# Last norm normalised on ScalarE, and other products that keep TensorE busy, in a perceiver layer kernel

## The reference

```python
x = x + xattn(_layernorm(x), ctx, ctx)    # 16 heads, 2048 context rows per batch, softmax
x = x + attn(_layernorm(x))               # gated scan over the tokens, state 64
x = x + ffn(_layernorm(x))                # 8 experts, top 2 of 8, and 2 shared experts

def _layernorm(x, axis=-1, eps=1e-05):
    m = jnp.mean(x, axis=axis, keepdims=True)
    v = jnp.var(x, axis=axis, keepdims=True)
    return (x - m) / jnp.sqrt(v + eps)
```

## Time and profile before

| | |
|---|---|
| time, median of 3 runs | 521.34 us (521.06 to 521.61) |
| the profiled execution | 521.11 us |
| its span, first to last instruction | 519.3 us |
| mean granted clock of TensorE | 0.974 |
| TensorE busy | 483.9 us (93%) |
| VectorE busy | 403.6 us (78%) |
| ScalarE busy | 332.4 us (64%) |
| POOL busy | 274.8 us (53%) |

### The profile page before, as it was taken

One profiled execution on the slowest core, in us unless ns is written; L12 is line 12 of the kernel. 1 busy time (PEld: TensorE's weight loads), 2 busy tenths in 40 slices (PEclk: granted clock), 3 DMA queues, 4 the chain that ended last, 5 costly groups with the idle time before them and its releaser, 6 DMA issues.

```text
span 519.3 us, 16078 instructions
## 1 busy us (share of the span) xinstructions
PE 483.9 (93%) x6871; PEld 343.7 (66%) x6871; DVE 403.6 (78%) x611; ACT 332.4 (64%) x371; POOL 274.8 (53%) x262
## 2 busy tenths in 40 slices
PE   4999879889999999999989999998999999999994
PEld 4456656566766676776766559645787878787642
DVE  3757867678877788878758787787899999989426
ACT  3356677567767668766575267464788988878310
POOL 0438887998999999999960213461010111100051
PEclk9759989999999999999999999999999999999998
DMA  6998957899897988889989220278999999997144
GB/s 225 245 290 229 248 155 230 237 269 251 208 272 247 265 261 259 221 223 319 328 314 359 74 82 2 66 258 326 394 366 416 418 419 418 416 414 290 40 122 142
DMA packets 29822, 133.99 MB, mean 258 GB/s; under 512 B 6452, under 2 KB 6708, under 8 KB 18996
## 3 DMA queue, kind: packets, MB, share of 16 engines
q1 hardware_dynamic: 26072, 120.91, 71.6%
q0 software_dynamic: 3680, 12.06, 6.4%
HBM read 96.77 MB, written 11.01 MB: 208 GB/s over the span
## 4 chain that ended last, share of the span: by engine, by line
PE 54%; DVE 29%; issue 8%; DMA 4%; POOL 2%; ACT 2%; SPq 0%; DVEq 0%; ACTq 0%; POOLq 0%
DVE ws L832 10%; PE bank L1096 9%; PE bank L1156 9%; DVE mx L766 8%; PE bank L1141 7%; PE bank L1165 6%; DMA wst<-in_ffw 3%; PE bank L1231 3%; PE bank L1309 2%; PE bank L1307 2%; PE bank L1308 2%; POOL ps L682 2%; PE bank L1173 2%; DVE hf L1012 2%; DVE hl L1017 2%
## 5 line engine op out<-in xcount | busy, mean ns | idle before, releaser
L766 DVE TENSOR_REDUCE mx<-bank 128x1 f32<-128x512 f32 x240 | 154.9, 686 | 53.9 <-PE bank L1096 52.0
L508 ACT ACTIVATE pt<-bank 128x1024 f32<-128x1024 f32 x128 | 124.4, 1023 | 56.9 <-PE bank L1141 50.6
L682 POOL TENSOR_TENSOR ps<-pt 128x512 f32<-128x512 f32 x120 | 149.6, 1272 | 1.0 <-ACT pt L508 0.5
L832 DVE SCALAR_TENSOR_TENSOR ws<-wst,ws 128x2048 f16<-128x2048 f32 x51 | 116.7, 2309 | 2.6 <-ACT ws L564 2.5
L564 ACT ACTIVATE ws<-wst 128x2048 f16<-128x2048 f32 x48 | 90.5, 1904 | 5.0 <-DMA wst<-in_ffw 4.7
L1322 PE MATMUL bank<-xt,ws 128*128 128x128 f16 x480 | 81.2, 219 | 0.8 <-DVE hf L1012 0.8
L1324 PE MATMUL bank<-xt,ws 128*128 128x128 f16 x480 | 81.2, 219 | 0.0
L1323 PE MATMUL bank<-xt,ws 128*128 128x128 f16 x480 | 81.2, 219 | 0.0
L723 POOL DMA_DIRECT2D ys_rows<-xn x15 | 8.1, 543 | 121.4 <-ACT xn L639 121.4
L658 POOL TENSOR_TENSOR kl<-kt,kh 128x512 f16<-128x512 f32 x58 | 67.3, 1182 | 9.1 <-ACT kh L454 6.8
L1156 PE MATMUL bank<-pt,v 128*32 128x128 f32 x2048 | 70.0, 276 | 2.2 <-issue 2.2
(11 more groups left out here) (190 smaller groups left out, 763.5 us busy)
## 6 DMA issues: line engine op xcount, KB each, us to landing
wst<-in_ffw SPq DMA_DIRECT2D x51, 1024.0 KB, 10.8
kt<-in_keysT SPq DMA_DIRECT2D x16, 1024.0 KB, 6.2
v<-in_vals SPq DMA_DIRECT2D x16, 1024.0 KB, 9.1
kstk<-kh SPq DMA_DIRECT2D x88, 128.0 KB, 4.7
kstk<-kl SPq DMA_DIRECT2D x44, 128.0 KB, 3.2
wst<-kh SPq DMA_DIRECT2D x40, 128.0 KB, 4.7
xs_rows<-biases SPq DMA_DIRECT2D x15, 256.0 KB, 7.7
x_tok<-xs_rows POOLq DMA_DIRECT2D x15, 256.0 KB, 8.8
```

The costliest lines, as they stand in the source:

```text
L508: act.activation(pt[:, n % 4, :, :, :].rearrange("p j a t -> p (j a t)"), bank[:, 2 * (n % 2):2 * (n % 2) + 2, :].rearrange("p j n -> p (j ...
L682: pool.tensor_tensor(ps2[:, n % 4, :, :], pt[:, n % 4, 0, :, :], pt[:, n % 4, 1, :, :], ALU.add)\
L766: dve.tensor_reduce(mx[:, a, q:q + 1], bank[:, 4 + k % 2, :], AX.X, ALU.max).then_inc(m_taken, 1)
L832: dve.scalar_tensor_tensor(ws[:, home_of(q), 1, m, :, :].rearrange("p c n -> p (c n)"), wst[:, q % 2, m, :, :].rearrange("p c n -> p (c n) ...
```

## The change

The last norm's tile is no longer made by VectorE. VectorE computes the reciprocal of the root and, in a new small operation, minus the mean times it, and signals a new semaphore. A new function normalise(b) on ScalarE waits for it and computes the tile as Identity(scale * x2 + bias), both columns per token. It stands in ScalarE's list at the end of round b of the loop, behind root(b), take_residual(b + 2), in the last round the load of the exponent table, and copy_high(b - 1). The idle products ahead of the transposes go from 10, 6, 6 to 6, 3, 5. And in quarter 0 of group 2, between a tile of max scores and the first scores, TensorE does seven products of ones to a bank whose maxima have been taken.

```diff
@@ -601,6 +602,11 @@
             act.wait_ge(scan_out, b + 1)
             act.activation(x2[:, b, :], bank[:, 4 + b, :], ACT.Copy, scale=1.0 / WS).then_inc(x2_done, 1)
 
+        def normalise(b):
+            act.wait_ge(third_set, b + 1)
+            act.activation(xn[:, b, :], x2[:, b, :], ACT.Identity, bias=lnv[:, 3, b:b + 1],
+                           scale=lnv[:, 2, b:b + 1]).then_inc(h3_done, 1)
+
         take_residual(0)
         take_residual(1)
         for b in range(B):
@@ -611,6 +617,7 @@
                 act.activation(r1[:, 2, 0:2], eps[:, :], ACT.Exp)
             if b > 0:
                 copy_high(b - 1)
+            normalise(b)
         copy_high(B - 1)
@@ -920,8 +927,8 @@
         def third_norm(b):
             dve.wait_ge(roots, 11 + b)
             link(dve.reciprocal(lnv[:, 2, b:b + 1], lnv[:, 0, b:b + 1]))
-            dve.tensor_scalar(xn[:, b, :], x2[:, b, :], mv[:, b, 0:1], lnv[:, 2, b:b + 1], ALU.subtract,
-                              ALU.mult).then_inc(h3_done, 1)
+            dve.scalar_tensor_tensor(lnv[:, 3, b:b + 1], mv[:, b, 0:1], -1.0, lnv[:, 2, b:b + 1], ALU.mult,
+                                     ALU.mult).then_inc(third_set, 1)
@@ -1168,9 +1175,9 @@
-        def keep_busy(count):
+        def keep_busy(count, n=7):
             for _ in range(count):
-                pe.matmul(bank[:, 7, 0:P], one[:, :], one[:, :], start=True, stop=True)
+                pe.matmul(bank[:, n, 0:P], one[:, :], one[:, :], start=True, stop=True)
@@ -1187,6 +1194,10 @@
                 if p == 1 and a == 1 and i + 2 < G:
                     queries(i + 2)
+                if i == 2 and p == 0 and a == 0:
+                    j, k = tenants[1]
+                    pe.wait_ge(m_taken, MB * j + k - 1)
+                    keep_busy(7, 4 + k % 2)
                 scores(n)
@@ -1341,7 +1352,7 @@
             if b < 3:
-                idle_products(3, (10, 6, 6)[b])
+                idle_products(3, (6, 3, 5)[b])
             transpose_tokens(b)
```

More of the change, by code:

```diff
@@ L263, in build_program @@
     idw_done = sem("scaled_identity_done")
+    third_set = sem("third_norm_factors")
     x2_done = sem("x2_done")
```

## The result

| | before | after |
|---|---|---|
| time, median of 6 runs | 521.2 us (519.38 to 521.82) | 525.4 us (523.68 to 528.78) |
| ratio | 1 | 1.0091, 95% interval 1.0059 to 1.0123 |
| the profiled execution | 521.11 us | 524.64 us |
| its span | 519.3 us | 522.9 us |
| TensorE, VectorE, ScalarE, POOL busy | 483.9, 403.6, 332.4, 274.8 us | 482.4, 401.5, 335.3, 274.7 us |

The change makes the kernel slower by 0.9%, 4.7 us by the ratio, 4.2 us between the medians. I had said 524.3 us (522.3 to 526.4), so the time lies in the range, 1.1 us above the forecast.

A forecast was written before the change was run, and what follows sets the result against it. The chain from the last norm through TensorE and VectorE's router was taken to bound the end; 521.11 + 2.1 (ring and table load) + 0.9 (clock) + 0 = 524.1, 524.3 us on the median's scale, range 522.3 to 526.4.

The forecast's parts named there:

- The ring and the table load: Last norm: ScalarE's normalise waiting on copy_high and transposes, plus the exponent table load, make batch 3's transposes 2.1 us later.
- Its split: Of the last norm's 2.1 us about 1.4 is table load and small activation, copy ahead of normalise(3) most of the rest.
- The fewer idle products: Last norm: transposes of batch 0 start 0.24 us earlier; otherwise fewer idle products cost nothing.
- The clock in the last norm: Last norm: a clock fall may follow TensorE's 2.3 us hole, costing 0 to 1.5 us, taken as 0.9.
- The third group, no gain: Third group: ones may speed TensorE by 1.2 to 1.5 us, but POOL's row bounds the stretch, so gain 0.
- The sign that I had named: Third group: TensorE waits for POOL near 75.5 for over 2 us instead of 1.02.
- The third group, the backlash: Third group: TensorE idles some 2.5 us before 75.51 and the clock falls behind it, about +1.1 us; chance 0.18.
- One for one behind the logits: Behind the last norm: a shift of the router's logits goes through in full, with nothing found to take it back.
- The sum: Whole kernel: 521.11 + 2.1 + 0.9 + 0 = 524.1 us, 524.3 on the median's scale.
- The forecast case: One fall of the clock, in the last norm, on top of the 2.1 us shift: 524.3 us, chance 0.38.
- rival 2: Clock falls both in the last norm and behind 75.51 in the third group: 525.4 us, chance 0.18.

The follow-up runs named there:

- norm_only: The whole change without the products of ones in the third group, with idle products 10, 6, 6 as before; 524.54 us, ratio to before 1.0060.
- load_behind: The whole change with the small exponent that loads the table moved behind the last normalisation; ratio to before 1.0071.
- filled: The whole change with ten idle products added ahead of the last transposes, in TensorE's last hole; 525.91 us, ratio to before 1.0102.
- ones_only: The kernel before with only the seven products of ones in the third group added; 523.64 us, ratio to before 1.0059.

## Why the prediction was right, and where it was not

- **The ring and the table load (2.1 us).** Right in size: 2.06 us in the same trace. normalise was 0.805 us where I had 0.82 from two neighbours' rows, the transposes 2.04 us apart where I had 2.06. ScalarE's last normalisation began 0.19 us after the step I gave, 0.04 us before it once the 0.23 us of the attention are taken off. norm_only shows that it is this part.
- **Its split.** Wrong: I gave the load 1.4 of the 2.1 us. load_behind measured 0.84. I had counted the load's whole length, and forgotten that the copy behind it has to wait for the transposes of batch 2 anyway. My own steps held this: those transposes end near 318.22, so the copy could not start before 318.25, and the load moved it to 319.13, 0.88 us.
- **The fewer idle products.** Right in sign. They bring 0.14 us with the norm on ScalarE, where I had 0.24 for batch 0, and 0.61 with the norm on VectorE.
- **The clock in the last norm (0.9, bounds 0 to 1.5).** In the profiled execution it fell behind a hole of 2.23 us (I had 2.3), 0.35 us behind its end and not 1.0, and cost 1.44 us at the logits, inside the bounds. At the chosen experts only 0.39 us of it was left. With the same hole it did not fall in norm_only, and filling the hole brought nothing in the median. As a term of the median 0.9 was too much.
- **The third group, no gain.** Right: 8.12 us to the queries of group 4 with and without the ones, bound by POOL. But the ones did not do what I had them do: in five of seven traces the clock was low before they began. The sign that I had named, over 2 us of waiting for POOL, did not come in after (1.18 us), and came in filled (2.58).
- **The third group, the backlash.** I had it as a rival at 0.18 and 1.1 us. One trace, filled, shows it, and with 3.0 us. The ones alone cost 2.2 to 3.1 us in the median. This is the term that was missing: my sum had 0 for the ones. Their 0.12 us of length was mis-sized too where they run at the low clock (3.1 to 3.4 us for 1.55), though POOL's lateness covers that. Why they cost so much is not settled: the cost is that of some executions, not of each. A fall behind the queries and VectorE's L795 caught by POOL have each been seen once, and whether taking L795 away lowers the cost is not clear of the noise.
- **One for one behind the logits.** Wrong between the logits and the experts, right behind them. There the router's two products wait for POOL's operations, so a shift of the logits is kept (filled, norm_only), cut by 1.06 us (after) or by 0.49 (load_behind), by how the two engines meet; I had said that POOL's low rows shift with the rest and keep their place, which held only where the clock stayed up and the order was as before. From the chosen experts to 436 us the shift stays, 2.67 to 2.73. What the block stages add between 436 and 480 us differs from trace to trace.
- **The sum.** 524.3 against 525.4. The time came out in the range partly by luck. The forecast case, one fall in the last norm, is what the profiled execution shows, yet that fall was worth 0.4 us at the experts and not 0.9. The median is rather the ring's 2.1 and some 2 to 3 us of the ones, for which the sum had nothing. 525.4 is also the number of rival 2, with both falls, but no trace shows both.

## What to carry to other kernels

Where a step moves to another engine, write down that engine's list in order and follow one item round: if the moved step waits for something that hangs on its own last result, two overlapped engines have become a ring (2.04 us a batch here, 1.78 before), and an engine's idle time elsewhere does not help. A table load is free only while its engine would be waiting anyway, so put it behind the last step that another engine waits for: here that was worth 0.84 us. Products added to keep the clock up lowered the time of no kernel here. Before adding them, look whether the clock is still up where they start, whether another engine bounds the stretch, and what hole follows behind it. And read a shift at the last place where another engine can take it up: 1.44 us at the logits were 0.39 at the experts.

## What the runs showed of the hardware

- A single VectorE operation (tensor_scalar) on SBUF of 128x512 took 0.55 us with POOL idle, 1.05 to 1.29 us beside POOL in groups 5 and 9, and once 7.15 us, as long as POOL's back-to-back operations went on. Two VectorE products of 32 elements took 0.98 and 1.08 us beside POOL, 0.19 alone; beside POOL each ended 0.04 or 0.05 us behind one of POOL's operations.
- The clock fell around holes of TensorE of 1.69 us (before), 2.23 (after), 2.27 (ones_only) and 2.58 (filled), and stayed up behind others of 2.23 us (norm_only), 1.39 us (load_behind, last norm) and 2.38 us (load_behind, at 53.3 us): with holes of this length it fell in some executions and not in others, and one execution's trace can't price it.
- An Identity activation of 128x512 from SBUF with columns for scale and bias took 0.805 us, and needed no table load of its own between the roots.
